# Attention value products of a head group: first key tile one round later, the other three together in the round behind it

## The chip, the cores and the metric

The kernel runs on one core of one Trainium2 chip. The metric is the device time of one launch in microseconds. A core has five engines that run their own instruction streams and meet only through semaphores: TensorE (PE, with its weight loads as PEld), VectorE (DVE), ScalarE (ACT), GpSimd (POOL) and SyncE (SP), which only issues DMAs here. Each engine takes its instructions in the order in which the program wrote them.

## The reference

Sixteen sequences of 512 tokens with 128 features pass through one block: attention, then a mixture of experts. What matters here is the attention:

```python
x = L0_attn_x                                  # (16, 512, 128)
Q = x @ W_q + b_q; K = x @ W_k + b_k; V = x @ W_v + b_v      # of layernorm(x)
# 16 heads of 8 features
scores = einsum('bhqd,bhkd->bhqk', Qh, Kh)
scores = (scores + einsum('bhqd,qkd->bhqk', Qh, rel_k)) / sqrt(8)
scores = where(causal, scores, -1e9)
attn = softmax(scores, axis=-1)
out = einsum('bhqk,bhkd->bhqd', attn, Vh) + einsum('bhqk,qkd->bhqd', attn, rel_v)
x = x + layernorm(out @ W_o + b_o)
x = x + layernorm(shared SwiGLU expert + top 2 of 8 routed experts, of layernorm(x))
```

## The kernel before

**Two stages.** The attention of all 16 sequences comes first (19 steps, to some 700 us of the profile), then the experts (`ffn_steps`), which the change does not touch.

**Steps and rounds.** In step t, four stages work at once on four sequences: stage F (normalise, queries, keys) on sequence t, A (the row maxima of the scores) on t-1, B (the exponentials and the value products) on t-2, C (the rest of the attention's output) on t-3. A and B meet in the steps t = 2 to 16, so 15 steps have both; step 17 has B and C alone. A step has 20 rounds (`ROUNDS`); rounds 5g to 5g+4 belong to group g of four heads (two pairs), and `u` is the round's place in its group, 0 to 4.

**Units.** In each round TensorE computes two units of transposed scores for the exponentials (e0 to e39 in a step, queries along the columns) and two units of scores for the maxima (s0 to s39). A unit fills one PSUM bank of 512 columns with one or two causal blocks of a head; `E_UNITS` and `S_UNITS` (lines 37 and 38) list them. The two halves of a round are s unit 2r and e unit 2r, then e unit 2r+1 and s unit 2r+1 (lines 1758 to 1779). Behind them `s_masks` (L1532 to L1542) adds the mask to both s units, and only its last two matmuls signal `s_full`: the pair of s units of a round is published together.

**Rings.** There are three banks for each kind (`ps_s`, `ps_e`; `RING = 3`). A unit may start when the use three places before it in the ring has been read: for s5 that is s2. The values product and the output projection take a place in the s ring behind s9 and s19 (so s15 has the bank of s12, s24 that of s21, s34 that of s31, s35 that of s32); the transposes of the input and of the output, the queries and the keys take one in the e ring.

**Who reads them.** ScalarE turns each e unit into `prob` (L799). VectorE takes the maximum of each s unit (L1127). GpSimd zeroes the masked part of `prob`, five masks a group (L640, `mask_tiles`), in between its normalisations and other work; its step is a fixed list (`masks(0, 1)`, ... in `step`, lines 677 to 716).

**Value products.** `av_part` (lines 1544 to 1559) multiplies `prob` of one key tile kt with the values of the four heads into `ps_av`, four matmuls of 512 - 128 kt columns (each shows as two instructions, x8 in the trace). Those of group g-1 are issued in the rounds of group g, behind the round's scores; those of group 3 in group 0 of the next step. It waits until all five masks of the group are done (L1546); with kt = 0 also until ScalarE has copied the group before out of `ps_av` (L1549). The last matmul of kt = 3 signals `av_full`. On that signal ScalarE copies `ps_av` to `av_s` (L864) and later the exponentials of group g+1 may overwrite `prob`.

**Other work in the rounds.** Ahead of a round's scores stand the uses of the table `AT` (line 44), for example: the sums for the near keys in round 1 (L1610, L1611), a transpose of `av_s` (L1563) in rounds 2, 6, 10 and 17, the maxima's transpose and the values product in round 5, the output's transpose in round 8, the queries in round 9 (L1578), the projection and the keys in round 10 (L1603, L1583), the transpose of the normalised row in round 18 (L1563 of `y`, which waits for VectorE's L1178 on the bank and GpSimd's L624 on `y`) and the logits in round 19 (L1644).

**VectorE's order.** Also a fixed list (`step`, lines 1282 to 1351): behind s0 the maxima of the second half, behind s1 and s20 and s30 statistics (L1085, L1090), behind s3, s10, s23, s35 the reading of a group's value sums (L1176, L1178), behind s9 the values (L1108, L1111).

**GpSimd's order around group 3.** The masks of groups 2 are followed by the normalisation L619 to L624, which waits for the statistics that VectorE makes behind s30, and whose result round 18's transposes read.

The order of TensorE's value products is the dictionary at line 1782. There is no planner: the order is written out by hand.

Of the kernel before, what the change touches and what calls it, by code (L numbers as in the profile page):

```python
# [222 lines left out]
def block_kernel(nc, x, W_q, b_q, W_k, b_k, W_v, b_v, W_o, b_o, rel_k, rel_v,  # L223
                 router_w, router_bias, sw1, sw3, sw2, ew1, ew2, out):
    ctx = ExitStack()
    with ctx:  # L226
# [1241 lines left out]
        def _(pe):  # L1468
# [97 lines left out]
            def x_transpose(st):  # L1566
                u = e_bank(st, "xT")

                pe.wait_ge(S["xn_ready"], st.at(st.f + 1, 1))
                transposes(lambda i: u[:, i * P:i * P + P], lambda i: xn[:, i, :], ident[:, :], S["e_full"])  # L1570
# [14 lines left out]
            def values(st):  # L1585
                u = s_bank(st, "v0")
                for i in range(NT):
                    last = pe.matmul(u[:, i * P:i * P + P], xnT[:, 1 + i * P:1 + i * P + P], wv[:, :],
                                     start=True, stop=True)
                last.then_inc(S["s_full"], 1)  # L1590

            def o_transpose(st):
                u = e_bank(st, "oT")

                pe.wait_ge(S["o_ready"], st.at(2 * (st.c + 1), 2))
                transposes(lambda i: u[:, i * P:i * P + P], lambda i: o_tok[:, i, :], ident[:, :], S["e_full"])

            def o_proj(st):
                u = s_bank(st, "oproj")

                pe.wait_ge(S["e_done"], st.e_use("oT")[0] + 1)
                for i in range(NT):
                    last = pe.matmul(u[:, i * P:i * P + P], oT[:, i * P:i * P + P], wo[:, :], start=True, stop=True)  # L1603
                last.then_inc(S["s_full"], 1)

            def e_sums(st):
                m = misc(st, "e_sums")

                pe.wait_ge(S["e_ready"], st.at(2 * (st.a + 1), 2))
                pe.matmul(m[0:32, :], head_sum[:, :], e0[:, :], start=True, stop=True)  # L1610
                pe.matmul(m[32:64, :], head_sum[:, :], e1[:, :], start=True, stop=True).then_inc(S["misc_full"], 1)  # L1611

            def s_tok_transpose(st):
                m = misc(st, "s_tok")

                pe.sem_inc(passed["pe"], 1)
                transposes(lambda i: m[:, i * 64:i * 64 + 64], lambda i: s_rows[:, i * P:i * P + P],
                           ident[0:64, 0:64], S["misc_full"])

            def m_transpose(st, s, half):  # L1620
                m = misc(st, f"m{half}")[:, :].bitcast(F16)

                pe.wait_ge(S["m16_ready"], st.at(2 * s + half + 1, 2))
                transposes(lambda i: m[0:H // 2, i * P:i * P + P], lambda i: m16[:, i, half * 8:half * 8 + 8],
                           ident16[:, :], S["misc_full"])

            def av_transpose(st, s, g):
                m = misc(st, f"av{g}")

                pe.wait_ge(S["av_copied"], st.at(NGRP * s + g + 1, NGRP))  # L1630
                transposes(lambda i: m[:, i * P:i * P + P], lambda i: av_s[g % 2][:, i * P:i * P + P],
                           ident[:, :], S["misc_full"])
# [96 lines left out]
            def step(st):  # L1729

                uses = {"av2": lambda: av_transpose(st, st.c, 2), "e_sums": lambda: e_sums(st),
                        "m1": lambda: m_transpose(st, st.b, 1), "s_tok": lambda: s_tok_transpose(st),
                        "av3": lambda: av_transpose(st, st.c, 3), "v0": lambda: values(st),
                        "oT": lambda: o_transpose(st), "xT": lambda: x_transpose(st), "oproj": lambda: o_proj(st),
                        "q": lambda: queries(st), "k": lambda: keys(st), "av0": lambda: av_transpose(st, st.b, 0),
                        "m0": lambda: m_transpose(st, st.a, 0), "av1": lambda: av_transpose(st, st.b, 1),
                        "xn2": lambda: xn2_transpose(st), "logits": lambda: logits(st)}
                if st.t0 == 1:
                    pe.wait_ge(S["const_ready"], N_CONST)
                    pe.wait_ge(S["rolled"], 2)  # L1740
                    pe.wait_ge(S["masked_made"], 4)

                    pe.matmul(ps_av[:, 0:P], bias_v[:, :], wo[:, :], start=True, stop=True).then_inc(S["bias_full"], 1)
                if st.t0 == 2:
                    pe.wait_ge(S["bias_ready"], 1)
                here = {"F": st.F, "A": st.A, "B": st.B, "C": st.C}
                if st.t0 == NSEQ + 2:
                    gate_transposes(True)
                for r in range(ROUNDS):
                    g, u = r // NU, r % NU  # L1750
                    for what, use in uses.items():
                        if AT[what] == r and here[STAGE[what]]:
                            if st.t0 == NSEQ + 2 and what == "xn2":
                                first_units(st)
                            use()
                    both = [None, None]

                    if st.A:
                        both[1] = s_unit(st, 2 * r)
                        s_part(st, 2 * r, both[1], 0)  # L1760
                    if st.B:
                        exps = e_unit(st, 2 * r)
                        e_part(st, 2 * r, exps, 0)
                    for n in range(1, len(E_UNITS[u])):
                        if st.A:
                            s_part(st, 2 * r, both[1], n)
                        if st.B:
                            e_part(st, 2 * r, exps, n)
                    if st.B:
                        exps = e_unit(st, 2 * r + 1)  # L1770
                        e_part(st, 2 * r + 1, exps, 0)
                    if st.A:
                        both[0] = s_unit(st, 2 * r + 1)
                        s_part(st, 2 * r + 1, both[0], 0)
                    for n in range(1, len(E_UNITS[u])):
                        if st.B:
                            e_part(st, 2 * r + 1, exps, n)
                        if st.A:
                            s_part(st, 2 * r + 1, both[0], n)
                    if st.A:  # L1780
                        s_masks(u, both)
                    for kt in {1: (0,), 2: (1, 2,), 3: (3,)}.get(u, ()):
                        if g > 0 and st.B:
                            av_part(st, st.b, g - 1, kt)
                        if g == 0 and st.C:
                            av_part(st, st.c, NGRP - 1, kt)
# [43 lines left out]
```

## Time and profile before

| what | value |
| --- | --- |
| time, median of 3 runs | 1042.57 us (1038.13 to 1042.66) |
| the profiled execution's own time | 1041.57 us |
| its span, first to last instruction | 1039.8 us |
| attention with all stages at work | about 140 to 660 us |
| experts alone | from about 780 us |
| mean granted clock of TensorE | 0.953 of full speed |

The span in 40 slices of 26 us, as busy tenths of each engine and the granted clock of TensorE:

```profile
PE   2778989989999899998998999888779999999995
...
DVE  5677788888888888889887888886468788878884
ACT  2137677767686777677767777665447767676763
POOL 4135676966867768668678686476247889898886
PEclk9759899999999999999999999997789999999999
```

How to read it: the digits are shares of a slice in tenths, 9 is 90% or more. From slice 6 to slice 25 the attention repeats; the dip around slices 27 to 30 is where the maxima have ended and the experts have not yet begun. In a timeline, a row names the start, the length, the engine and line, the output and input tiles and how many instructions are merged (x8); in square brackets stands the idle time of the engine just ahead of it and who ended it. The clock row is read as a share of 2.4 GHz; the two levels are 1.2 and 2.4 GHz.

### The profile page before, as it was taken

The page shows a single profiled execution, that of the slowest core. Times are in us where ns is not written, and L with a number is a line of the kernel's source. Part 1 is how long each engine was busy: PE and PEld are TensorE (multiplying, and loading weights), DVE is VectorE, ACT ScalarE, POOL GpSimd, SP SyncE. Part 2 cuts the span into 40 slices and gives each one's busy share as a digit, 9 for nine tenths or more (in the row PEclk, how much of TensorE's full clock was granted, in tenths as well). Part 3 has the DMA queues.
Part 4 walks back from the last instruction along what each step waited for, and adds up shares of the span by engine and source line. Part 5 has one row for each costly group of instructions (what it writes and reads, how often), then busy time and mean ns, then how long its engine had stood idle before and what let it go on. Part 6 is the DMA issues. An engine that isn't in the chain of part 4 may idle for free. (4 is left out here: it accounts for less than half of the span.)

```text
span 1039.8 us, 23478 instructions
## 1 busy us (share of the span) xinstructions
PE 908.0 (87%) x7655; PEld 513.8 (49%) x7655; DVE 834.4 (80%) x1948; ACT 678.6 (65%) x1305; POOL 725.9 (70%) x940
## 2 busy tenths in 40 slices
PE   2778989989999899998998999888779999999995
PEld 0324444444444444444444444432457777777773
DVE  5677788888888888889887888886468788878884
ACT  2137677767686777677767777665447767676763
POOL 4135676966867768668678686476247889898886
PEclk9759899999999999999999999997789999999999
DMA  2610111101111101011011010102325454545541
GB/s 48 169 45 28 36 41 33 50 33 40 44 34 44 43 32 50 31 43 48 31 44 41 32 49 32 42 13 56 136 67 168 147 162 150 171 150 165 165 139 31
DMA packets 64004, 74.93 MB, mean 72 GB/s; under 512 B 10032, under 2 KB 39600, under 8 KB 63904
## 3 DMA queue, kind: packets, MB, share of 16 engines
q1 hardware_dynamic: 61536, 73.17, 22.1%
q10 hardware_dynamic: 2368, 0.48, 0.5%
q8 instruction: 56, 0.92, 0.4%
q14 instruction: 44, 0.36, 0.1%
HBM read 43.75 MB, written 8.65 MB: 50 GB/s over the span
## 5 line engine op out<-in xcount | busy, mean ns | idle before, releaser
L1127 DVE TENSOR_REDUCE mx<-ps_s 128x1 f32<-128x512 f32 (+2 forms) x640 | 408.9, 682 | 81.6 <-PE ps_s L1539 79.9
L799 ACT ACTIVATE prob<-ps_e 128x512 f32<-128x512 f32 x640 | 347.0, 600 | 122.3 <-PE ps_e L1496 122.3
L640 POOL TENSOR_SCALAR_AFFINE_SELECT prob<-prob 128x516 f32<-128x516 f32 (+1 forms) x320 | 173.7, 568 | 173.5 <-ACT prob L799 173.5
L1518 PE MATMUL ps_s<-ks,qs 63*128 63x512 f16 (+3 forms) x1024 | 226.8, 312 | 34.8 <-DMA ks<-kl 13.6
L1496 PE MATMUL ps_e<-qs,ks 64*128 64x512 f16 (+3 forms) x1024 | 213.7, 307 | 7.5 <-ACT prob L799 4.6
L1555 PE MATMUL ps_av<-prob,vp 128*32 128x512 f32 (+3 forms) x2048 | 185.3, 458 | 22.7 <-POOL prob L640 22.5
L721 POOL TENSOR_TENSOR hidden_low<-hidden,hidden_high 128x512 fp32r<-128x512 f32 x144 | 191.2, 1357 | 11.9 <-ACT hidden_high L988 10.7
L1518 PEld LDWEIGHTS ps_s<-ks,qs 63*128 63x128 f16 x1024 | 64.5, 95 | 162.9 <-DVE mx L1127 84.1
L988 ACT CAST hidden_high<-hidden 128x512 fp32r<-128x512 f32 x160 | 98.0, 613 | 30.4 <-DVE hidden L1440 27.2
L1539 PE MATMUL ps_s<-masked_at,below_r 64*128 64x128 bf16 (+3 forms) x640 | 108.7, 211 | 0.0
L1539 PE MATMUL ps_s<-masked_at,below 64*128 64x130 bf16 (+3 forms) x640 | 93.5, 213 | 0.0
L1496 PEld LDWEIGHTS ps_e<-qs,ks 64*128 64x128 f16 x1024 | 68.9, 95 | 38.0 <-ACT prob L799 26.5
L1440 DVE TENSOR_TENSOR hidden<-gate_rows,ps_e 128x512 f32<-128x512 f32 x96 | 64.1, 683 | 28.6 <-ACT ps_e L1004 28.4
L1555 PEld LDWEIGHTS ps_av<-prob,vp 128*32 128x32 f32 x2048 | 47.7, 110 | 71.6 <-POOL prob L640 30.5
L1705 PE MATMUL ps_av<-hidden_high,w_high 128*128 128x512 f32 x160 | 69.3, 433 | 9.4 <-POOL hidden_low L721 9.3
L1539 PEld LDWEIGHTS ps_s<-masked_at,below_r 64*128 64x128 bf16 x640 | 60.9, 98 | 20.1 <-issue 2.2
L1004 ACT ACTIVATE ps_e<-ps_e 128x512 f32<-128x512 f32 x96 | 55.8, 582 | 20.4 <-PE ps_e L1672 19.8
L1705 PE MATMUL ps_av<-hidden_high,w_low 128*128 128x512 f32 x160 | 63.1, 394 | 0.0
L1705 PE MATMUL ps_av<-hidden_low,w_high 128*128 128x512 f32 x160 | 62.8, 393 | 0.0
L1539 PEld LDWEIGHTS ps_s<-masked_at,below 64*128 64x128 bf16 x640 | 52.9, 97 | 14.5 <-issue 2.0
L1563 PEld LDWEIGHTS ps_misc<-ident,av_s 128*128 128x128 f32 x256 | 28.6, 148 | 49.0 <-issue 46.8
L622 POOL TENSOR_TENSOR rs<-var,neg_half 128x4 f32<-128x4 f32 x48 | 48.9, 1020 | 3.8
(176 smaller groups left out, 1746.2 us busy)
## 6 DMA issues: line engine op xcount, KB each, us to landing
gate_rows<-gates_dram SPq DMA_DIRECT2D x128, 256.0 KB, 3.5
qs<-qh SPq DMA_DIRECT2D x128, 32.0 KB
qs<-ql SPq DMA_DIRECT2D x128, 32.0 KB
xnT_dram<-oT SPq DMA_DIRECT2D x16, 256.0 KB, 2.0
xeT<-xnT_dram SPq DMA_DIRECT2D x16, 256.0 KB, 2.7
out<-result SPq DMA_DIRECT2D x16, 256.0 KB, 2.3
v_near<-v_back SPq DMA_DIRECT2D x16, 254.0 KB
ks<-kh SPq DMA_DIRECT2D x124, 32.0 KB
```

Source lines behind the costliest of these rows:

```text
L640: pool.affine_select(out=v, in_=v, compare_op=ALU.is_ge, fill=0.0, base=-2, pattern=cols, channel_multiplier=-1).then_inc(S["p_masked"], 1)
L721: pool.tensor_tensor(hidden_low[hid(f, i)][:, :].bitcast(F32R), hidden[hid(f, i)][:, :], hidden_high[hid(f, i)][:, :], ALU.subtract).then_ ...
L799: act.activation(prob[g % 2][:, u, b, :], ps_e[bank][:, :], ACT.Exp, scale=SCALE).then_inc(S["e_done"], 1)
L988: act.copy(hidden_high[hid(f, i)][:, :].bitcast(F32R), hidden[hid(f, i)][:, :]).then_inc(S["high_ready"], 1)
L1004: act.activation(front[k % 4][:, :], front[k % 4][:, :], ACT.Gelu).then_inc(S["act_ready"], 1)
L1127: dve.tensor_reduce(out, src, AX.X, ALU.max).then_inc(s_free[bank], 1)
L1440: dve.tensor_tensor(hidden[hid(f, i)][:, :], gate_rows[:, k, :], front[k % 4][:, :], ALU.mult).then_inc(S["hidden_ready"], 1)
L1496: last = pe.matmul(scores[:, at:at + WIDTH[kt]], ks[par][rows, pr, P * kt:P * kt + P], qs[par][rows, pr, P * kt:SEQ], start=True, stop=True)
L1518: pe.matmul(scores[:, at:at + P * (qt + 1)], qs[par][rows, 2 * g + off, P * qt:P * qt + P], ks[par][rows, 2 * g + off, 0:P * (qt + 1)], st ...
L1539: last = pe.matmul(diagonals(both[b], u, part), (below if b == part else below_r)[rows, :], columns, start=False, stop=(part == 1))
L1555: last = pe.matmul(ps_av[32 * j:32 * j + 32, P * kt:SEQ], vp[par][:, kt, 4 * g + j, :], prob[g % 2][:, u, j % 2, at:at + w], start=(kt == ...
L1705: last = pe.matmul(ps_av[:, :], ws[:, w, :].bitcast(F32R), hs[hd][:, :].bitcast(F32R), start=(i % n == 0 and j == 0), stop=(i % n == n - 1 ...
```

## The change

The dictionary that says which key tiles' value products stand behind which round of a group is changed. Before: tile 0 behind round u = 1, tiles 1 and 2 behind u = 2, tile 3 behind u = 3. After: tile 0 behind u = 2, tiles 1, 2 and 3 behind u = 3. Nothing else differs.

```diff
@@ -1779,7 +1779,7 @@
                             s_part(st, 2 * r + 1, both[0], n)
                     if st.A:
                         s_masks(u, both)
-                    for kt in {1: (0,), 2: (1, 2,), 3: (3,)}.get(u, ()):
+                    for kt in {2: (0,), 3: (1, 2, 3,)}.get(u, ()):
                         if g > 0 and st.B:
                             av_part(st, st.b, g - 1, kt)
                         if g == 0 and st.C:
```

## Rows read from the trace of the kernel before

**Rows 1.** The page's part 1: busy us (share), instructions
```profile
PE 908.0 (87%) x7655; PEld 513.8 (49%) x7655; DVE 834.4 (80%) x1948; ACT 678.6 (65%) x1305; POOL 725.9 (70%) x940
```

**Rows 2.** Waits, 140 to 620 us: who waited: total us, times, longest
```profile
PEld ps_s L1518 <- DVE mx L1127: 57.5, 135, 1.6
DVE mx L1127 <- PE ps_s L1539: 44.8, 77, 2.3
...
PE ps_av L1555 <- POOL prob L640: 17.0, 22, 0.9
```

**Rows 3.** PE timeline, four steps: start us, us, what [idle before]
```profile
232.72 0.63 PE L1563 MATMUL ps_misc<-ident,y 128*128 128x128 f32 x4 [0.50 <-DVE num L1178]
...
270.28 1.93 PE L1555 MATMUL ps_av<-prob,vp 128*32 128x512 f32 x8 [0.89 <-POOL prob L640]
...
316.24 0.66 PE L1563 MATMUL ps_misc<-ident,y 128*128 128x128 f32 x4 [0.44 <-DVE num L1178]
...
357.54 0.65 PE L1563 MATMUL ps_misc<-ident,y 128*128 128x128 f32 x4 [0.44 <-DVE num L1178]
```

**Rows 4.** Stretches near 271 us: length, PE busy, granted clock, DMA
```profile
266.50:270.00 3.50, 2.74 (x31) 1.00 0.13 47
270.00:273.40 3.40, 3.12 (x16) 0.53 0.18 55
```

**Rows 5.** PE timeline, rounds 1 to 4 of one step, group 0
```profile
323.02 1.06 PE L1555 MATMUL ps_av<-prob,vp 128*32 128x512 f32 x8 [0.64 <-POOL prob L640]
324.02 0.66 PE L1563 MATMUL ps_misc<-ident,av_s 128*128 128x128 f32 x4
...
325.04 0.28 PE L1518 MATMUL ps_s<-ks,qs 63*128 63x256 f16 x1
...
325.48 1.28 PE L1555 MATMUL ps_av<-prob,vp 128*32 128x384 f32 x16
326.69 0.39 PE L1518 MATMUL ps_s<-ks,qs 63*128 63x512 f16 x1
...
327.29 0.43 PE L1555 MATMUL ps_av<-prob,vp 128*32 128x128 f32 x8
327.65 0.33 PE L1518 MATMUL ps_s<-ks,qs 63*128 63x384 f16 x1
...
328.14 0.33 PE L1518 MATMUL ps_s<-ks,qs 63*128 63x384 f16 x1
```

**Rows 6.** DVE timeline beside rows 5
```profile
324.31 1.27 DVE L1127 TENSOR_REDUCE mx<-ps_s 128x4 f32<-128x512 f32 x2
...
326.66 3.26 DVE L1127 TENSOR_REDUCE mx<-ps_s 128x2 f32<-128x512 f32 x5
330.76 0.69 DVE L1108 TENSOR_TENSOR v_back<-ps_s,dv 128x512 f32<-128x512 f32 x1 [0.84 <-PE ps_s L1539]
```

**Rows 7.** PE timeline, round 7, group 1
```profile
334.90 0.28 PE L1518 MATMUL ps_s<-ks,qs 63*128 63x256 f16 x1
```

**Rows 8.** DVE timeline beside rows 7, to round 10
```profile
333.56 2.52 DVE L1127 TENSOR_REDUCE mx<-ps_s 128x1 f32<-128x512 f32 x4
...
343.38 0.69 DVE L1127 TENSOR_REDUCE mx<-ps_s 128x1 f32<-128x512 f32 x1 [0.56 <-PE ps_s L1539]
```

**Rows 9.** PE timeline, round 12, group 2
```profile
304.72 0.28 PE L1518 MATMUL ps_s<-ks,qs 63*128 63x256 f16 x1 [0.39 <-DVE mx L1127]
```

**Rows 10.** DVE timeline, rounds 10 to 17, groups 2 and 3
```profile
304.01 1.85 DVE L1127 TENSOR_REDUCE mx<-ps_s 128x1 f32<-128x512 f32 x3
...
307.67 3.15 DVE L1127 TENSOR_REDUCE mx<-ps_s 128x1 f32<-128x512 f32 x5 [0.34 <-PE ps_s L1539]
...
314.62 1.29 DVE L1127 TENSOR_REDUCE mx<-ps_s 128x2 f32<-128x512 f32 x2 [0.71 <-PE ps_s L1539]
```

**Rows 11.** PE timeline, round 16, group 3
```profile
312.27 1.07 PE L1555 MATMUL ps_av<-prob,vp 128*32 128x512 f32 x8 [0.89 <-POOL prob L640]
```

**Rows 12.** POOL timeline, the normalisation ahead of round 18
```profile
314.83 1.04 POOL L624 TENSOR_TENSOR y<-y,rs 128x512 f32<-128x512 f32 x1
```

## The prediction

> **What bounds the kernel now.** I read the page first. TensorE is the busiest engine and VectorE stands close behind it [rows 1], so neither can be called the bound from shares alone. The change touches only the attention stage, so I turned to the waits of twelve of its repeating steps. Three of them matter [rows 2]: TensorE stood idle 17.0 us for the causal masks of GpSimd ahead of the value products; VectorE's maxima stood idle 44.8 us for scores; and TensorE's weight loads for scores were held 57.5 us in 135 waits by VectorE, which had not yet emptied a bank. The last two go in opposite directions: TensorE and VectorE take turns at being late, through a ring of three banks. A step lasts 357.54 - 316.24 = 41.30 us [rows 3]. The timelines then say who is late where, and the path that sets the step's length has to be followed through both engines, in program order.
>
> **What the change moves.** No instruction is added or removed, on any engine or queue. Per group of heads, the first key tile's products leave round u=1 and stand behind round u=2, and those of tiles 1 and 2 leave round u=2 and stand with tile 3 behind round u=3. The lengths on TensorE, from start to next start: tile 0 takes 324.02 - 323.02 = 1.00 us, tiles 1 and 2 take 326.69 - 325.48 = 1.21 us, tile 3 takes 327.65 - 327.29 = 0.36 us [rows 5]. So what stands behind rounds 1, 2, 3 goes from 1.00, 1.21, 0.36 to 0, 1.00, 1.57 us. The last product of a group is in the same place, so the copy of ps_av, the reuse of prob and all later work find their signal in the same order; I cost these at nothing, covered by whole rounds of score work between them. Nothing is queued anew behind a wait: the mask wait of tile 0 only moves back a round. SP's queue is passed by nothing.
>
> **The gain.** Two of the four waits per step for GpSimd are idle time: 0.89 us in group 3's round 16 [rows 11] and 0.64 us in group 0's round 1 [rows 5]. A round later the masks are done, so both vanish as such. Whether the time is won depends on what TensorE meets next.
>
> **Group 0.** Behind the removed products TensorE meets s4 and s5 of round 2. With three banks, s5 needs the bank of s2. VectorE ends s2 about 0.65 us into the pair that starts at 324.31 [rows 6], so at 324.96, and s5 starts at 325.04 [rows 5]: today it already starts as soon as VectorE permits. VectorE's own chain up to s2 has no wait for those products. So the 1.00 us of tile 0 and the 0.64 us wait, 1.64 us together, become an idle stretch in front of s4 and s5. From s5 on TensorE is the late one: it runs on without a pause to the values product, for which VectorE waits 0.84 us [rows 6]. On that stretch the change takes off 0.21 us (1.21 - 1.00), then adds 1.21 us (1.57 - 0.36). In round 4, s9 waits today for the bank of s6: s8 to s9 takes 0.49 us [rows 5], where the same rounds without such a wait take some 0.25 us less; this cover falls away, - 0.25. Sum + 0.75 us. The lump outlasts VectorE's store, which is two published units: 2 x 0.63 us = 1.26 us (five take 3.15 us [rows 10]), while 1.57 us plus the next round's scores stand ahead of the next publication.
>
> **Group 1.** s15 needs the bank of s12, the second of four reductions from 333.56 [rows 8], so free at about 334.82, and s15 starts at 334.90 [rows 7]: again VectorE's pace. From there TensorE sets the pace until VectorE waits 0.56 us in round 10 [rows 8]. - 0.21 + 1.21 = + 1.00 us.
>
> **Group 2.** s24 waits 0.39 us for s21 [rows 9], the first of the three from 304.01 [rows 10]. The tile 0 products before it hide nothing; without them the wait is 1.39 us. Then, as in group 0, round 14 is published 0.75 us later, and VectorE, which now runs through from 307.67 [rows 10], is starved for it: + 0.75 us.
>
> **Group 3.** Here the gain is real: VectorE waits 0.71 us in round 17 [rows 10], and TensorE's wait for the masks is the cause. New, round 17's pair can be published when s32's bank is free plus some 0.5 us, just as VectorE ends s33; the 0.71 us goes, and cancels group 2's 0.75 us but for 0.04. Then the transposes ahead of round 18 wait today for VectorE, until 316.24 [rows 3]. What is late next is GpSimd's normalisation, which ends at 314.83 + 1.04 = 315.87 [rows 12]; it starts from VectorE's statistics, now later, and ends some 0.67 us later, at 316.54: + 0.30 in place of + 0.04. Behind round 18 stands the lump: + 1.21. Groups 2 and 3 together: + 1.51 us.
>
> **Sum.** 0.75 + 1.00 + 1.51 = + 3.26 us a step. Score and value work meet in 15 steps; in the first of them other things are late (loads, a slow clock), so I take 14: + 45.6 us. The last step with values has no maxima and gets 0.
>
> **The clock.** In two of the twelve steps the granted clock fell for a stretch: 0.53 as the mean of 270.00 to 273.40 [rows 4], thus 1.2 GHz for most of it, from 2.4. Before it TensorE had stood idle 0.89 us, and the products behind that took 1.93 us [rows 3] against 1.07 [rows 11]. Such a fall costs 316.24 - 232.72 - 2 x 41.30 = 0.92 us [rows 3]. The new order has idle stretches of that size at four places a step, so I estimate some 3 falls more, + 2.8 us; the bounds are none (0) and one in every step (15 x 0.92 = 14 us).
>
> Forecast: 45.6 + 2.8 = + 48.4 us on the profiled execution's own 1041.57 us, 1090.0 us. That execution stands 1.0 us below the median of the runs, 1042.57 us, within their spread. A measurement here can tell some 0.5%, or 5 us, from no change.
>
> By the Trainium skill ("TensorE: Matmul & The Clock Gate", section "A second HAM failure mode: psum-queue depth-cycling"), a TensorE that pauses often between groups of matmuls as it cycles through PSUM banks swings between its two clocks. The trace shows two such falls in twelve steps with short pauses in all of them; if the rule ruled here, the sum would stand at its upper bound for the clock.
>
> **Rivals.** (1) *TensorE alone is the bound*, faster. Then the idle removed is won: 17.0 us over 480 us is 1.46 us a step, x 15 = 22 us, 1019.6 us. For it: 87% busy [rows 1] and a plain wait. Against it: s5, s15 and s24 start within 0.1 us of VectorE's release, so only one of the two waits stands ahead of work that could start. It decides if VectorE's releases were not what those starts waited for. Chance 0.07. The Trainium skill ("Perfetto Trace Analysis", section "Optimization Strategy") would side with this rival: find the gaps on the busiest engine and let what they wait for be there sooner. The trace agrees on which engine that is, not on what follows.
> (2) *The lump is mostly covered*, no change: VectorE has a backlog where I see it starving, and 0.71 us of gain in group 3 meets an equal loss. 1040 to 1046 us. Against it stands that it waits already today at 307.67 and 330.76 behind smaller lumps [rows 6, 10]. Chance 0.04.
> (3) *Half of it*: the lumps' ends overlap the next scores, or other waits absorb some; 1.6 us a step x 14 = 22 us, 1064 us. Chance 0.14.
> (4) *The clock gives way in every step*: + 15 x 3.26 + 14 = 63 us, 1104 us; several falls a step would give more, 1115. Chance 0.13.
> (5) That the edit does not act can be left out: the tuple of key tiles is read by TensorE's program alone, and each tile's products follow it.
>
> **How the numbers follow.** The forecast, about 3 us a step, has 0.62. Its own range is 1075 to 1100. To hold 8 in 10, the range takes in the half case and most of the clock case: 1062 to 1110 us. Faster by over 0.5%: 0.07. Within 0.5%: 0.04. Slower: 0.14 + 0.13 + 0.62 = 0.89.
>
> **What the changed profile would show.** A step of some 44.5 us. No idle time of TensorE put down to the masks ahead of the value products. In its place, waits for VectorE of over 1 us at the first score product of rounds 2, 7 and 12. VectorE's waits for scores up from 44.8 us per twelve steps by some 39 us, in the rounds behind the lump (4, 9, 14, 19), 1.5 to 2 us each. The mean granted clock a little lower, and the FFN stage behind it as long as before. I am wrong if round 2's scores start earlier than VectorE's chain allows here, if VectorE does not wait in rounds 4 and 14, or if the step stays at 41 us.

## The result and the profile after

The changed kernel takes 1085.95 us (median of 4 runs, 1081.85 to 1088.44) against 1042.07 us: a ratio of 1.044, 95% interval 1.0408 to 1.0472. It is slower, by 43.9 us. (The kernel before now has four runs, hence 1042.07 in place of 1042.57 us.) The profiled execution took 1081.85 us, 40.3 us above that of before; it is the fastest of the four, with a mean granted clock of 0.949 against 0.933 to 0.939 in the other three. One execution of a later kernel (1582.48 us, where its other ten took 1032.7 to 1038.5) is left out of that kernel's ratio.

The page's part 1 of the changed kernel, beside [rows 1]: the same instructions and nearly the same busy times, in a longer span.

```profile
PE 905.7 (84%) x7655; PEld 520.9 (48%) x7655; DVE 817.1 (76%) x1948; ACT 678.2 (63%) x1305; POOL 725.1 (67%) x940
```

Waits of 140 to 620 us, the columns as in [rows 2]. The wait for GpSimd's masks ahead of the value products (17.0 us before) is gone from the list. VectorE's wait for scores went from 44.8 to 85.4 us, TensorE's matmuls wait 33.5 us for VectorE's release of a bank (4.9 us before), and its weight loads 94.5 us against 57.5. Steps are longer now, so the same window holds fewer of them.

```profile
PEld ps_s L1518 <- DVE mx L1127: 94.5, 168, 1.8
...
DVE mx L1127 <- PE ps_s L1539: 85.4, 82, 1.9
PE ps_s L1518 <- DVE mx L1127: 33.5, 48, 1.7
...
PE ps_misc L1563 <- POOL y L624: 11.4, 10, 1.1
```

TensorE's timeline of one step, from the transposes ahead of round 18 to the same a step later, in which the clock did not fall. The step is 416.24 - 372.62 = 43.62 us, against 41.30 us [rows 3].

```profile
372.62 0.63 PE L1563 MATMUL ps_misc<-ident,y 128*128 128x128 f32 x4 [1.14 <-POOL y L624]
...
381.73 0.28 PE L1518 MATMUL ps_s<-ks,qs 63*128 63x256 f16 x1 [0.51 <-DVE mx L1127]
...
382.16 1.06 PE L1555 MATMUL ps_av<-prob,vp 128*32 128x512 f32 x8
...
383.76 1.50 PE L1555 MATMUL ps_av<-prob,vp 128*32 128x384 f32 x24
385.19 0.33 PE L1518 MATMUL ps_s<-ks,qs 63*128 63x384 f16 x1
...
385.43 0.32 PE L1518 MATMUL ps_s<-ks,qs 63*128 63x384 f16 x1
...
391.74 0.28 PE L1518 MATMUL ps_s<-ks,qs 63*128 63x256 f16 x1 [0.80 <-DVE mx L1127]
...
404.31 0.28 PE L1518 MATMUL ps_s<-ks,qs 63*128 63x256 f16 x1 [1.38 <-DVE mx L1127]
...
416.24 0.63 PE L1563 MATMUL ps_misc<-ident,y 128*128 128x128 f32 x4 [1.15 <-POOL y L624]
```

In group 0, s5 starts at 381.73 after an idle 0.51 us, tile 0 stands at 382.16, and tiles 1 to 3 take 385.19 - 383.76 = 1.43 us in one stretch. The new waits for VectorE's banks stand where they were looked for: 0.51 us ahead of s5 in round 2, 0.80 us ahead of s14 in round 7, and 1.38 us ahead of s24 in round 12. Ahead of round 18 it is now GpSimd that ends the idle time.

VectorE in the same step: maxima (L1127) and, at 378.99 and 379.26, the small operations of the second half's maxima.

```profile
376.96 1.90 DVE L1127 TENSOR_REDUCE mx<-ps_s 128x4 f32<-128x512 f32 x3 [1.79 <-PE ps_s L1539]
...
378.99 0.24 DVE L1154 SCALAR_TENSOR_TENSOR m<-mx,s_best 128x32 f16<-128x32 f32 x1
379.26 0.43 DVE L1158 TENSOR_TENSOR d<-s_tok,m 128x32 f32<-128x32 f32 x2
...
381.00 1.27 DVE L1127 TENSOR_REDUCE mx<-ps_s 128x4 f32<-128x512 f32 x2
...
385.96 1.29 DVE L1127 TENSOR_REDUCE mx<-ps_s 128x4 f32<-128x512 f32 x2 [0.76 <-PE ps_s L1539]
...
388.20 0.69 DVE L1108 TENSOR_TENSOR v_back<-ps_s,dv 128x512 f32<-128x512 f32 x1 [0.95 <-PE ps_s L1539]
...
398.21 1.29 DVE L1127 TENSOR_REDUCE mx<-ps_s 128x4 f32<-128x512 f32 x2 [1.86 <-PE ps_s L1539]
...
401.67 0.69 DVE L1127 TENSOR_REDUCE mx<-ps_s 128x1 f32<-128x512 f32 x1 [0.56 <-PE ps_s L1539]
...
409.14 1.91 DVE L1127 TENSOR_REDUCE mx<-ps_s 128x4 f32<-128x512 f32 x3 [0.81 <-PE ps_s L1539]
...
412.27 3.10 DVE L1127 TENSOR_REDUCE mx<-ps_s 128x1 f32<-128x512 f32 x5
```

It starves behind the lumps: 1.79 us in round 19, 0.76 in round 4, 0.95 at the values, 1.86 in round 9, 0.81 in round 14. The row at 401.67 is its first maximum of round 10, a mark that is used below. In round 17 it now runs through (five reductions from 412.27), where it stood 0.71 us before [rows 10].

The whole step in one row, after and then before (us, then busy time and count of PE, PEld, DVE, ACT, POOL, granted clock, DMA share, GB/s):

```profile
372.60:416.20 43.60, 37.14 (x408) 18.97 (x408) 34.76 (x91) 30.29 (x60) 30.47 (x46) 1.00 0.11 38
```

```profile
316.20:357.50 41.30, 37.64 (x408) 18.48 (x408) 36.17 (x91) 30.36 (x60) 30.57 (x46) 1.00 0.12 40
```

Both have 408 matmul instructions. No engine is busy for longer but the weight loads (18.97 against 18.48 us); VectorE is even busy 1.4 us less. The 2.3 us are idle time.

The clock accounts for the rest. From 149.88 to 682.31 us lie twelve steps, 532.43 us, 9.0 us more than 12 x 43.62; before, twelve steps took 497.36 us, 1.8 us more than 12 x 41.30. Steps of some 45.0 us alternate with steps of 43.6 to 43.9 us in the changed kernel, six of each. In a long step, TensorE idles 1.39 us and the products behind run at the lower clock (1.93 us against 1.06 at 382.16); the stretch around it (length, busy, granted clock) shows 0.79 on average, between 1.2 and 2.4 GHz:

```profile
536.59 0.28 PE L1518 MATMUL ps_s<-ks,qs 63*128 63x256 f16 x1 [1.39 <-DVE mx L1127]
...
537.94 1.93 PE L1555 MATMUL ps_av<-prob,vp 128*32 128x512 f32 x8
```

```profile
534.00:539.00 5.00, 3.32 (x32) 0.79 0.06 20
```

One long step has a second fall right behind the first (281:284 us, granted clock 0.50). It is no longer than the others (45.14 us), and the step behind it takes 43.72 us, so that fall cost hardly anything.

So 12 steps account for 35.1 us: 27.8 us of step and 7.2 us of clock. The remaining 5.2 us of the 40.3 all lie behind these twelve steps: they begin at the same time in both kernels (150.05 and 149.88 us), and the three steps behind them take 118.4 us against 112.9.

### The profile page after: what moved, and what is told of

Same layout as the page of the kernel before. It is cut to its first block and busy times, and to the rows that moved or that the text cites. A ratio compares the mean times of both kernels' runs of the same rounds, so it can differ in the third digit from the quotient of the medians.

```text
span 1080.1 us, 23478 instructions
## 1 busy us (share of the span) xinstructions
PE 905.7 (84%) x7655; PEld 520.9 (48%) x7655; DVE 817.1 (76%) x1948; ACT 678.2 (63%) x1305; POOL 725.1 (67%) x940
## 5 line engine op out<-in xcount | busy, mean ns | idle before, releaser
L1127 DVE TENSOR_REDUCE mx<-ps_s 128x1 f32<-128x512 f32 (+2 forms) x640 | 408.8, 682 | 138.0 <-PE ps_s L1539 136.6
L1496 PE MATMUL ps_e<-qs,ks 64*128 64x512 f16 (+3 forms) x1024 | 220.3, 311 | 12.0 <-ACT prob L799 5.5
L1555 PE MATMUL ps_av<-prob,vp 128*32 128x512 f32 (+3 forms) x2048 | 176.1, 463 | 0.0
L1539 PE MATMUL ps_s<-masked_at,below_r 64*128 64x128 bf16 (+3 forms) x640 | 106.1, 214 | 0.0
L1555 PEld LDWEIGHTS ps_av<-prob,vp 128*32 128x32 f32 x2048 | 54.4, 111 | 51.0 <-issue 30.9
L1539 PEld LDWEIGHTS ps_s<-masked_at,below 64*128 64x128 bf16 x640 | 49.9, 99 | 14.7 <-issue 2.3
L1563 PE MATMUL ps_misc<-ident,av_s 128*128 128x128 f32 x256 | 42.9, 291 | 11.8 <-ACT av_s L864 5.9
```

Of the source, the lines that this page charges most:

```text
L1127: dve.tensor_reduce(out, src, AX.X, ALU.max).then_inc(s_free[bank], 1)
L1496: last = pe.matmul(scores[:, at:at + WIDTH[kt]], ks[par][rows, pr, P * kt:P * kt + P], qs[par][rows, pr, P * kt:SEQ], start=True, stop=True)
L1539: last = pe.matmul(diagonals(both[b], u, part), (below if b == part else below_r)[rows, :], columns, start=False, stop=(part == 1))
L1555: last = pe.matmul(ps_av[32 * j:32 * j + 32, P * kt:SEQ], vp[par][:, kt, 4 * g + j, :], prob[g % 2][:, u, j % 2, at:at + w], start=(kt == ...
```

## The experiments

All edits but two are to the one dictionary; one of the two is to one place in VectorE's order, the other to both. The diffs are shown against the kernel before. "Step" is a step without a fall of the clock that recurs, read from the transposes of `y` as above. Each ratio compares with runs of the kernel before that were taken along with it; their medians were 1040.28, 1038.47 and 1041.03 us from one set of experiments to the next, so that a difference of 0.3% says little by itself.

**One group at a time.** The new order in the rounds of one group, before's in the other three.

```diff
-                    for kt in {1: (0,), 2: (1, 2,), 3: (3,)}.get(u, ()):
+                    for kt in ({2: (0,), 3: (1, 2, 3,)} if g == 0 else {1: (0,), 2: (1, 2,), 3: (3,)}).get(u, ()):
```

*Group 0.* 

> The new order only in the rounds of group 0. Theory A (what stands on TensorE behind the last score unit that VectorE's release holds back lengthens the step; a step is 41.30 us before and 43.62 us after, where the clock does not fall): the products behind round 2 and 3 go from 1.21 + 0.36 to 1.00 + 1.43 us, less 0.25 us in round 4 and plus some 0.15 us through ScalarE; the three small two-input operations of VectorE at the start of the group still run beside GpSimd's masks and stay long (0.47, 0.57, 0.37 us), because group 3 is as before. So the step grows by 0.75 us, + 11 us for the run, 1053 us. Rival B (the 0.73 us by which VectorE's chain got shorter in the changed kernel came from the order in group 0 itself): step + 0.02 us, 1042 us.

Measured 1052.75 us, ratio 1.0123 (1.0100 to 1.0147). The step is 491.18 - 449.13 = 42.05 us, + 0.75.

Theory A's + 0.75 us. VectorE's small operations stayed long (0.47 and 0.94 us). Rival B is out.

*Group 1.* 

> The new order only in the rounds of group 1, where TensorE has no wait for GpSimd before. Theory A: -0.21 + 1.07 = + 0.87 us a step, + 13 us, 1055 us, and a wait of TensorE for VectorE of about 0.8 us ahead of round 7. Rival C (it is the masks' waits and their removal that matter, so groups without them show nothing): 1042 us.

Measured 1058.06 us, ratio 1.0162 (1.0129 to 1.0194). Step 449.18 - 407.02 = 42.16 us, + 0.87 as expected; the run is 3 us slower than expected, since long steps are frequent here too.

The waits for the masks are as before in this kernel (0.89 and 0.64 us), so it isn't their removal that costs: rival C is out.

*Group 2.* 

> The new order only in the rounds of group 2. Theory A: round 14 is published 0.6 us later, but round 17 waits for the masks of GpSimd in any case (0.89 us), which swallows it; what is left comes through the statistics and GpSimd's normalisation ahead of round 18: some + 0.4 us a step, + 6 us, 1048 us. Rival D (each lump costs the same wherever it stands): + 0.87 us a step, 1055 us.

Measured 1055.22 us, ratio 1.0147 (1.0122 to 1.0172). Step 407.22 - 365.27 = 41.95 us, + 0.64.

Between theory A's + 0.4 and rival D's + 0.87 us, and by time (15 us for 6 expected) well above theory A. The trace splits it. From VectorE's first maximum of round 10 to that of round 19 a step takes 17.84 us in place of 17.46: + 0.38, theory A's term. The other + 0.27 us stands in group 0, where the small operation L1154 now lasts 0.73 us in place of 0.47 (what these operations wait for is shown below). Theory A had not looked there. Every other step takes 43.4 us with a fall of the clock.

*Group 3.* 

> The new order only in the rounds of group 3. Theory A: round 17 comes 0.7 us earlier, of which only 0.2 us passes GpSimd's normalisation ahead of round 18; the lump behind round 18 adds 1.07 us; VectorE's three small operations at the start of group 0 now fall behind most of GpSimd's masks and get some 0.7 us shorter. Together + 0.2 us a step, + 3 us, 1045 us. If these operations are not shortened by that: + 0.87 us a step, 1055 us. The sum of the four single groups against the full change (+ 43.9 us) tells whether the parts add up: theory A expects 33 to 36 us of them, the rest being falls of the clock.

Measured 1039.4 us, ratio 1.001 (0.9992 to 1.0027). Step 436.22 - 394.80 = 41.42 us, + 0.11.

The small operations of VectorE in this kernel, one step:

```profile
401.18 0.26 DVE L1154 SCALAR_TENSOR_TENSOR m<-mx,s_best 128x32 f16<-128x32 f32 x1
401.47 0.44 DVE L1158 TENSOR_TENSOR d<-s_tok,m 128x32 f32<-128x32 f32 x2
```

The single one takes 0.26 us and the pair 0.44, against 0.47 and 0.94 us before (shown further below). From round 10 to round 19 the step grows by 0.82 us (18.28 in place of 17.46), and from round 19 to the values it shrinks by 0.71 (10.51 in place of 11.22). So the lump of group 3 and what it delays pay each other, as theory A had it. This kernel's trace also has one fall of the clock between 150 and 650 us, where before's has two.

The four steps add up: 0.75 + 0.87 + 0.64 + 0.11 = 2.37 us, against 2.32 us for the full change. That is in part luck: the 0.27 us that group 2 alone costs through L1154 is absent from the full change, and groups 2 and 3 cost 1.45 us there between round 10 and round 19, against 0.38 + 0.82 = 1.20 us alone.

**What counts, the place or the length of the stretch?** Tile 0 back, the other three together:

```diff
-                    for kt in {1: (0,), 2: (1, 2,), 3: (3,)}.get(u, ()):
+                    for kt in {1: (0,), 3: (1, 2, 3,)}.get(u, ()):
```

> Tile 0 back behind round u = 1, tiles 1, 2 and 3 together behind u = 3, in all groups. Theory A (only what stands behind the last score unit that VectorE's release holds back counts; here that unit moves into round 3, because the rounds 2 and 3 follow each other at once): + 0.4 us in group 0, - 0.1 in group 1, 0 in group 2, + 1.1 in group 3: a step of 42.7 us, about 1062 us. Rival E (the longest stretch without scores, 1.43 us against 1.21, is what starves VectorE, and tile 0 does nothing): as the full change or slower, a step of 43.6 us or more, 1076 us or more.

Measured 1067.58 us, ratio 1.0269 (1.0246 to 1.0292). Step 585.45 - 543.17 = 42.28 us, + 0.98 in place of + 1.4.

The lump alone, 1.43 us as in the full change, costs less than half of its 2.32 us. Rival E, for which tile 0 does nothing, is out. Theory A's places are right and its sum is not. In group 1 the step gets 0.14 us shorter, as expected, where the full change adds 0.85. But the expectation has no term for the start of group 0, where the way from round 19 to s2 gets 0.72 us shorter here too (table below). By time the kernel is 5.6 us over theory A; its clock falls in most steps.

```diff
-                    for kt in {1: (0,), 2: (1, 2,), 3: (3,)}.get(u, ()):
+                    for kt in {2: (0, 1, 2,), 3: (3,)}.get(u, ()):
```

> Tiles 0, 1 and 2 behind round u = 2 (some 2.1 us in one stretch), tile 3 behind u = 3 as before. Theory A: the same 1.00 us is carried behind the held round 2 as in the full change, and the long stretch itself costs little more: a step of 42.8 to 43.6 us, 1065 to 1080 us. Rival E (the longest stretch without scores decides): 2.1 us against 1.43 us in four groups, a step above 45 us, over 1095 us.

Measured 1082.35 us, ratio 1.0428 (1.0403 to 1.0453). Step 549.02 - 505.15 = 43.87 us; the shortest are 682.22 - 639.38 = 42.84 us.

The steps of 42.84 us come only right behind a step with a fall of the clock; two steps in a row at a granted clock of 1.00 (505 to 593 us) take 43.87 us each, 0.3 us above theory A's range. Against the full change's 43.62 us, a stretch of 2.14 us in place of 1.43 costs 0.11 us in group 0 and nothing in group 1. What counts is that the group's products stand behind round 2, and rival E (over 45 us) fails a second time. Seven of the twelve steps have a fall (44.3 to 46.5 us), which puts the time a little over theory A's too.

**A version that might beat both.** If work behind the held round costs and work ahead of it is free, tile 3 should move on, past round 19:

```diff
-                    for kt in {1: (0,), 2: (1, 2,), 3: (3,)}.get(u, ()):
+                    for kt in {1: (0,), 2: (1, 2,), 4: (3,)}.get(u, ()):
```

> Before's order, with tile 3 behind round u = 4 in place of u = 3. Theory A: in group 3 the round 19 is published 0.36 us earlier while VectorE waits for it (0.72 us), and the 0.36 us goes into a stretch in which VectorE holds TensorE back: a step of 40.9 us, 1037 us. In the other groups nothing. Rival E (spreading or lumping decides; here the stretches are as many and as long): 1042 us.

Measured 1044.78 us, ratio 1.0053 (1.0034 to 1.0072): slower, a step of 41.69 us. The expectation missed. Rows of ScalarE in group 0 and then of VectorE show what it had left out.

```profile
411.63 0.58 ACT L864 COPY av_s<-ps_av 128x512 f32<-128x512 f32 x1 [0.37 <-PE ps_av L1555]
...
413.07 0.56 ACT L845 COPY vp<-ps_s 128x512 f32<-128x512 f32 x1
```

```profile
403.96 0.64 DVE L1154 SCALAR_TENSOR_TENSOR m<-mx,s_best 128x32 f16<-128x32 f32 x1
404.63 0.93 DVE L1158 TENSOR_TENSOR d<-s_tok,m 128x32 f32<-128x32 f32 x2
...
406.87 1.27 DVE L1127 TENSOR_REDUCE mx<-ps_s 128x4 f32<-128x512 f32 x2
...
413.72 0.69 DVE L1108 TENSOR_TENSOR v_back<-ps_s,dv 128x512 f32<-128x512 f32 x1 [1.24 <-PE ps_s L1539]
```

TensorE's rows in group 0 complete them; [rows 5] ends ahead of the values product, which stood at 328.89 us there.

```profile
410.70 0.33 PE L1518 MATMUL ps_s<-ks,qs 63*128 63x384 f16 x1
...
411.13 0.43 PE L1555 MATMUL ps_av<-prob,vp 128*32 128x128 f32 x8
...
411.69 1.16 PE L1588 MATMUL ps_s<-wv,xnT 128*128 128x128 f32 x8
```

The values come 413.72 - 406.87 = 6.85 us behind s2's start in place of 330.76 - 324.31 = 6.45 us [rows 6], 0.40 us later. Two things make that up. First, s9 waits for VectorE's release of s6's bank, and starts 3.83 us behind s2 in both kernels (410.70 - 406.87, 328.14 - 324.31). Tile 3 used to stand ahead of that wait and now stands behind it, so the values product starts 411.69 - 406.87 = 4.82 us behind s2 in place of 328.89 - 324.31 = 4.58: + 0.24 us. This is theory A's own rule, which the expectation had not applied to round 4. Second, ScalarE's copy of `ps_av` stands in its fixed order ahead of its copy of the values (L845), and now it stands idle 0.37 us for the late tile 3. VectorE reads the values only when that copy has ended (413.07 + 0.56 = 413.63 us; it starts at 413.72, and the trace names TensorE as the releaser all the same): the other 0.16 us. In group 2 the same held unit stands in round 14, and the stretch from round 10 to round 18 grows by 0.25 us; group 1 gains 0.22. And the earlier round 19 brings VectorE's first small operation more time beside the masks: 0.64 us in place of 0.47. The gain ahead of round 19 was 0.21 us, in place of 0.36. So the held units, on the two engines that theory A follows, account for 0.49 us of the loss, the third queue for 0.16 and the small operation for 0.17.

In group 3 alone, with tiles 0 to 2 behind round 17:

```diff
-                    for kt in {1: (0,), 2: (1, 2,), 3: (3,)}.get(u, ()):
+                    for kt in ({2: (0, 1, 2,), 4: (3,)} if g == 3 else {1: (0,), 2: (1, 2,), 3: (3,)}).get(u, ()):
```

> Before's order in groups 0 to 2; in group 3 tiles 0, 1 and 2 behind round u = 2 and tile 3 behind u = 4. Theory A: no wait for the masks in round 16; round 18 comes 0.2 us earlier (then GpSimd's normalisation holds it), round 19 another 0.36 us: - 0.56 us a step, 40.7 us, 1034 us; perhaps a little lost again in group 0, if VectorE's small operations run beside more of GpSimd's masks. Rival E: a stretch of 2.1 us without scores in group 3, slower than before, 1050 us or more.

Measured 1035.61 us, ratio 0.9965 (0.9949 to 0.998). Step 437.27 - 396.19 = 41.08 us, - 0.2 in place of - 0.56.

It is the fastest of the kernels with another placement, 0.35% under before. That is less than the 0.5% that I had given a measurement, but its step is shorter too. Between round 10 and round 19 the step gains 0.47 us of the 0.56. In group 0 it loses 0.26 again: 0.10 in the small operations (L1154 0.32 us in place of 0.47, but the two subtractions L1158 1.19 in place of 0.94) and 0.16 behind s2, because TensorE, which arrives earlier, waits 1.10 us for the masks in round 1 in place of 0.64.

```profile
401.62 1.19 DVE L1158 TENSOR_TENSOR d<-s_tok,m 128x32 f32<-128x32 f32 x2
```

With tile 3 at its old place:

```diff
-                    for kt in {1: (0,), 2: (1, 2,), 3: (3,)}.get(u, ()):
+                    for kt in ({2: (0, 1, 2,), 3: (3,)} if g == 3 else {1: (0,), 2: (1, 2,), 3: (3,)}).get(u, ()):
```

> Before's order in groups 0 to 2; in group 3 tiles 0, 1 and 2 behind round u = 2, tile 3 behind u = 3 as before. Theory A: no wait in round 16, round 18 comes 0.2 us earlier, the rest as before: a step of 41.1 us, 1036 us; beside the kernel with tile 3 in u = 4 as well (step 41.10 us) it tells what the late tile 3 gave: 0.25 us expected by its own, less what VectorE's small operations lost beside more of the masks, so nearly the same. Rival E (a stretch of 2.1 us starves VectorE): slower than before.

Measured 1037.38 us, ratio 0.9976 (0.996 to 0.9993); the step is 41.32 us, the same as before, so by the step it missed 41.1. The expected gain is there, 17.21 us from round 10 to round 19 in place of 17.46, but group 0 takes it back: L1154 lasts 0.74 us in place of 0.47. The time is 0.24% lower all the same, which the step doesn't explain: this stays open, and at that size I take it for no difference. The 0.2 us by which the version above has the shorter step come with its late tile 3.

**VectorE's small operations beside GpSimd's masks.** The full change had made VectorE's chain 0.73 us shorter, unforeseen. To see why, the operations were moved on VectorE alone, past the masks:

```diff
                 maxima(0, 1)
-                if st.B:
-                    max_half(st, st.b, 1)
                 maxima(1, 2)
                 if st.F:
                     ln1_bn(st)
+                if st.B:
+                    max_half(st, st.b, 1)
                 maxima(2, 3)
```

> Before's order of the products; on VectorE the maxima of the second half (three small two-input operations, which last 0.47, 0.57 and 0.37 us beside GpSimd's masks) stand behind s1 and the statistics, when GpSimd's four masks have ended. Theory F (these operations are long because they run beside GpSimd's masks): they shrink to 0.2 to 0.3 us each at that place. The step gains only about 0.2 us, because GpSimd's masks release the first products of group 0 at nearly the same time: 1037 us. Rival G (the length belongs to the operations at this place in the step, whatever GpSimd does): they stay at 0.4 to 0.6 us and the time does not change.

Measured 1038.64 us, ratio 0.9992 (0.9975 to 1.0008), a step of 41.16 us. VectorE's two lines, then the four masks of GpSimd, which ended at 403.89, then TensorE's products:

```profile
403.85 0.19 DVE L1154 SCALAR_TENSOR_TENSOR m<-mx,s_best 128x32 f16<-128x32 f32 x1
404.07 0.29 DVE L1158 TENSOR_TENSOR d<-s_tok,m 128x32 f32<-128x32 f32 x2
```

```profile
401.89 2.00 POOL L640 TENSOR_SCALAR_AFFINE_SELECT prob<-prob 128x256 f32<-128x256 f32 x4
```

```profile
403.94 1.06 PE L1555 MATMUL ps_av<-prob,vp 128*32 128x512 f32 x8 [0.64 <-POOL prob L640]
```

The three operations take 0.19 us and 0.29 us for the pair. They are short where no mask runs beside them: theory F, and rival G is out. The time hardly moves, as expected, since TensorE still waits 0.64 us for the masks themselves.

The masks of the kernel before, taken one by one, say how long the operations are made:

```profile
321.33 0.68 POOL L640 TENSOR_SCALAR_AFFINE_SELECT prob<-prob 128x516 f32<-128x516 f32 x1
...
322.55 0.41 POOL L640 TENSOR_SCALAR_AFFINE_SELECT prob<-prob 128x256 f32<-128x256 f32 x1
```

L1154 starts at 321.56 beside the first of these and ends at 322.03, the mask at 322.01. The last subtraction ends at 322.07 + 0.94 = 323.01, the last mask at 322.96. It is so in every trace kept here: between 150 and 650 us, 632 of these operations took over 0.23 us, and every one ended 0.04 to 0.05 us behind the end of a mask. The other 303 either started within 0.16 us of the mask's end or had no mask beside them (33 of them, 0.18 to 0.19 us). So the length depends on where in a mask the operation starts, which is why a shift of VectorE by some tenths of a microsecond made L1154 0.19, 0.24, 0.47 or 0.73 us long.

> Both changes together: in group 3 tiles 0, 1, 2 behind u = 2 and tile 3 behind u = 4, and VectorE's maxima of the second half behind s1 and the statistics. Theory F: the 1.19 us of the two subtractions fall to some 0.5 us; the step goes to between 40.6 and 41.0 us (GpSimd's masks then hold group 0's first products): 1030 to 1035 us. Rival G: as without it, 41.1 us, 1036 us.

The same edit on top of the faster placement. Measured 1037.47 us, ratio 0.9969 (0.9955 to 0.9983). The subtractions fell to 0.43 us, but the step stayed at 41.1 us and the gain at 0.3%, short of the expected 1030 to 1035 us: rival G's number for another reason. TensorE waits 1.11 us for the masks in round 1 there; with VectorE ready earlier, GpSimd alone sets that place.

**The steps side by side.** Each step without a fall, cut at five marks: VectorE's first maximum of round 19, its maximum of s2, its reading of the values (L1108), its first maximum of round 10, TensorE's transposes ahead of round 18, and round 19 again. Microseconds.

| kernel | 19 to s2 | s2 to values | to round 10 | to round 18 | to round 19 | step |
| --- | --- | --- | --- | --- | --- | --- |
| before | 4.77 | 6.45 | 12.62 | 14.16 | 3.30 | 41.30 |
| full change | 4.04 | 7.20 | 13.47 | 14.56 | 4.35 | 43.62 |
| group 0 alone | 4.77 | 7.20 | 12.62 | 14.16 | 3.30 | 42.05 |
| group 1 alone | 4.78 | 6.45 | 13.48 | 14.16 | 3.30 | 42.17 |
| group 2 alone | 5.04 | 6.45 | 12.62 | 14.57 | 3.27 | 41.95 |
| group 3 alone | 4.06 | 6.45 | 12.62 | 13.94 | 4.35 | 41.42 |
| tile 0 back, lump | 4.05 | 7.02 | 12.48 | 14.38 | 4.34 | 42.28 |
| tiles 0 to 2 behind u = 2 | 5.03 | 7.31 | 13.48 | 14.79 | 3.27 | 43.87 |
| tile 3 behind u = 4 | 4.94 | 6.85 | 12.40 | 14.41 | 3.09 | 41.69 |
| group 3: 0 to 2 behind 2, 3 behind 4 | 4.87 | 6.61 | 12.62 | 13.94 | 3.05 | 41.10 |
| group 3: 0 to 2 behind 2, 3 behind 3 | 5.03 | 6.45 | 12.62 | 13.94 | 3.27 | 41.32 |

## Why the prediction was right

It said 1090.0 us; the median is 1085.95 us. The mechanism held; the sizes partly cancelled, and one of its own signs of being wrong came up (below). The parts, per step. In the full change group 0 is the stretch from VectorE's first maximum of round 19 to the values (11.24 in place of 11.22 us), group 1 that from the values to round 10 (13.47, 12.62), groups 2 and 3 that from round 10 to round 19 (18.91, 17.46). The last column is the growth of the whole step when one group alone is changed:

| step of the prediction | predicted | in the full change | group alone |
| --- | --- | --- | --- |
| group 0 | + 0.75 | + 0.02 | + 0.75 |
| group 1 | + 1.00 | + 0.85 | + 0.87 |
| groups 2 and 3 | + 1.51 | + 1.45 | + 0.64 and + 0.11 |
| sum | + 3.26 | + 2.32 | + 2.37 |
| clock, whole run | + 2.8 us | + 7.2 us in twelve steps | |

**Where TensorE is held.** Right, in all four groups. The masks' wait vanished and did not come back as time, since s5, s15 and s24 could not start before VectorE's release: new idle time of 0.51, 0.80 and 1.38 us stands there. I had expected 1.64 us in round 2 and 1.39 in round 12, and over 1 us in all three, so one of three came out. In round 2, 0.73 us of the shortfall of 1.13 is VectorE's earlier release (below). In round 7 nothing of tile 0's 1.00 us was won either: s14 starts 3.54 us behind the values in both kernels (391.74 - 388.20 us; 334.30 - 330.76 before). VectorE's waits in rounds 4, 9, 14 and 19 were to be 1.5 to 2 us each; they are 0.76 (and 0.95 at the values), 1.86, 0.81 and 1.79.

**The lump.** Right in place, too large in size. I added 1.00, 1.21 and 0.36 us as they stood in the trace of before; the three tiles in one stretch take 1.43 us and not 1.57. So the lump adds 1.07 us instead of 1.21, 0.14 us less in three places.

**Group 0.** Here a term was missing. The chain from round 19 to s2 was taken as fixed, and "round 2's scores start earlier than VectorE's chain allows here" was given as a sign of being wrong. It came up: s5 starts 381.73 - 376.96 = 4.77 us behind round 19's first maximum, before 325.04 - 319.54 = 5.50. The chain itself became 0.73 us shorter: from 376.96 to 381.00 is 4.04 us, from 319.54 to 324.31 it had been 4.77. VectorE's chain at that place in the kernel before, and above it [rows 6] for s2:

```profile
319.54 1.91 DVE L1127 TENSOR_REDUCE mx<-ps_s 128x4 f32<-128x512 f32 x3 [0.72 <-PE ps_s L1539]
...
321.56 0.47 DVE L1154 SCALAR_TENSOR_TENSOR m<-mx,s_best 128x32 f16<-128x32 f32 x1
322.07 0.94 DVE L1158 TENSOR_TENSOR d<-s_tok,m 128x32 f32<-128x32 f32 x2
```

The single operation takes 0.47 us against 0.24 after, the pair 0.94 against 0.43. In the changed kernel the lump of group 3 delays them until half of GpSimd's masks are through, and they start nearer to a mask's end. In the other direction ScalarE's busy queue brought the values 0.16 us later: their product starts 0.59 us later behind s2 (5.17 in place of 4.58 us), VectorE reads them 0.75 us later (7.20 in place of 6.45). With group 0 changed alone the chain stayed as it was, and the predicted + 0.75 us came out to the hundredth. That is luck: the lump was 0.14 us shorter than I had it, and ScalarE's 0.16 us, which I had at nothing, made up for it.

**Groups 2 and 3.** Right: the 0.71 us of the mask wait was won, group 2's delay took it back, GpSimd's normalisation became what ends the idle time ahead of round 18 (1.15 us), and the lump behind it was paid in full. Here two errors met: the normalisation cost 0.41 us for 0.30, the lump 0.14 less.

**The clock.** Mis-sized. I gave it three falls more at 0.92 us; there were seven in twelve steps against two, and six of them cost 9.0 / 6 = 1.5 us each. It isn't that the slowed products now stand on the path and did not before. The fall at 560 us of the kernel before shows it:

```profile
549.89 0.69 DVE L1127 TENSOR_REDUCE mx<-ps_s 128x1 f32<-128x512 f32 x1 [0.56 <-PE ps_s L1539]
...
568.92 1.91 DVE L1127 TENSOR_REDUCE mx<-ps_s 128x4 f32<-128x512 f32 x3 [0.72 <-PE ps_s L1539]
...
579.33 0.69 DVE L1108 TENSOR_TENSOR v_back<-ps_s,dv 128x512 f32<-128x512 f32 x1 [0.84 <-PE ps_s L1539]
```

From round 10 to round 19 it takes 19.03 us in place of 17.46, so the fall cost 1.57 us there, about as much as it does now. But the delay brings VectorE's small operations past most of the masks (0.19 and 0.41 us in place of 0.47 and 0.94), and the way to the values takes 10.41 us in place of 11.22: 0.81 us comes back. In the changed kernel these operations are short already and little can come back: the stretch with the fall grows by 1.44 us (533.95 to 554.30), and the next to the values keeps its 11.24.

The rule of the Trainium skill ("TensorE: Matmul & The Clock Gate", section "A second HAM failure mode: psum-queue depth-cycling") fits the direction: more short pauses, more falls; in no run here did every step have one.

**The rivals.** TensorE alone as the bound would have given a gain from the removed waits. The kernels of groups 0 and 1 refute it: with group 0's wait removed the step grew by 0.75 us. That the Trainium skill ("Perfetto Trace Analysis", section "Optimization Strategy") sends one to the gaps of the busiest engine is right as a place to look; the traces agree on that, not on closing them as such: in group 3 it paid 0.25 us of 0.89 (the version with tiles 0 to 2 behind u = 2 and tile 3 behind u = 3, from round 10 to round 19), in group 0 nothing. The half case (1064 us) lies outside what was measured. The overestimate of the step, 14 x 0.94 = 13 us, was partly made up by the clock and by the three steps behind the twelve; so the total came nearer than its terms. This account is of the profiled execution, which grew by 40.3 us where I had 48.4. The medians lie 43.9 us apart; what the other three executions added is not in a trace, but their clock was lower.

## What to carry to other kernels

Before removing a wait in an in-order engine, look at the next instruction behind it: if that one is held by a ring of buffers, the wait was free, and whatever is moved past the held instruction is paid in full. Ask this at every round, not only at the one that the change is about: the late tile 3 cost what it should have won because another unit, two rounds on, was held as well. Follow the path through every queue that has a fixed order, the slower ones too: here a copy on ScalarE and a normalisation on GpSimd each took part of a gain that the two busiest engines promised. When pieces are merged, take the length of the merged piece as a range, and ask which small operations of other engines will now run beside something else.

## What the runs showed of the hardware that I had not expected

Small VectorE operations with two operands in SBUF that start while GpSimd runs a mask over SBUF last until that mask has ended: a 128 x 32 subtraction takes 0.18 to 0.19 us alone and up to 0.68 us beside a mask, the scaled maximum 0.19 us against up to 0.75. Their length thus depends on where in the mask they start, and an unrelated delay of some tenths of a microsecond can shorten or lengthen them by half a microsecond. Beside the same masks the maxima, which read PSUM, kept their 0.69 us, and the reduction L1151 of one operand in SBUF its 0.17 us. The Trainium skill ("SBUF — State Buffer", section "Who interferes with whom") says that a VectorE instruction with two inputs in SBUF shares its second read interface with GpSimd; the traces agree (0.47 us for two operands, 0.17 for one, in the same stretch of masks).

The falls of the clock are not spread evenly: in the changed kernel every other step has one, behind an idle stretch of 1.39 us in round 12, while the step between, with the same idle stretch (1.38 us), has none. Why one and not the other was not tried.
